# A stack of four graph layers on one core: ScalarE applies layer 2's normalisation too, and the guard of the row sums becomes the bias of their square root

## What is computed

```python
x = _layernorm(x + _L0(x, adj, nodemask, ...))   # two-layer MLP of ((1+eps) x + aggregated x)
x = _layernorm(x + _L1(x, adj, adj, ...))        # relu([x, aggregated x / deg] @ W + b)
x = _layernorm(x + _L2(x, adj, ...))             # below
x = _layernorm(x + _L3(x, adj, ...))             # MLP per edge, normalised, summed over the edges

# _layernorm:  (x - mean) / sqrt(var + eps)
# _L2:
adj_self = adj + I
rowsum = adj_self.sum(axis=2)                    # deg + 1
d = rowsum ** (-0.5);  d = where(isinf(d), 0, d)
out = (adj_self * d[:, :, None] * d[:, None, :]) @ (x @ weight) + bias
```

## Time and profile before

| | |
|---|---|
| runs shown | 545.76 us median of 3 (543.46 to 546.49) |
| the profiled execution | 544.14 us, its span 542.4 us |
| mean granted TensorE clock | 0.976 |
| busy, share of the span | PE 89%, PEld 76%, DVE 86%, ACT 66%, POOL 74% |
| instructions | PE 3299, DVE 1739, ACT 904, POOL 603 |
| first part | from the start to about 256 us |
| second part | from there to the end, a store of `out` every 8.4 us in the middle |

### The profile page before, as it was taken

One profiled execution on the slowest core, in us unless ns is written; L12 is line 12 of the kernel. 1 busy time (PEld: TensorE's weight loads), 2 busy tenths in 40 slices (PEclk: granted clock), 3 DMA queues, 4 the chain that ended last, 5 costly groups with the idle time before them and its releaser, 6 DMA issues. The chain is left out here.

```text
span 542.4 us, 13404 instructions
## 1 busy us (share of the span) xinstructions
PE 480.5 (89%) x3299; PEld 413.0 (76%) x3299; DVE 465.3 (86%) x1739; ACT 356.6 (66%) x904; POOL 401.6 (74%) x603
## 2 busy tenths in 40 slices
PE   3689998989899895975799999999999999999992
PEld 3568777778777774863689889888888888888881
DVE  5699999999999998994378998888888888888886
ACT  2256666766676673765477877776777767777773
POOL 4466666666666653644879999999999999999963
PEclk9999999999999997999699999999999999999996
DMA  5124444434333333212211222213212222122111
GB/s 187 59 70 128 127 127 128 126 126 126 126 119 118 110 121 122 75 63 90 73 49 45 89 75 57 77 55 86 76 54 77 57 83 77 53 78 60 53 40 40
DMA packets 50641, 47.49 MB, mean 88 GB/s; under 512 B 5424, under 2 KB 42288, under 8 KB 50608
## 3 DMA queue, kind: packets, MB, share of 16 engines
q1 hardware_dynamic: 50608, 47.12, 28.2%
HBM read 28.22 MB, written 18.87 MB: 87 GB/s over the span
## 5 line engine op out<-in xcount | busy, mean ns | idle before, releaser
L1353 PEld LDWEIGHTS bank<-w2c,hE 128*128 128x128 f32 x512 | 67.4, 192 | 2.0
L567 POOL TENSOR_TENSOR AD<-AD,dis 128x256 f32<-128x256 f32 x32 | 19.6, 614 | 64.6 <-DVE dis L940 64.6
L1353 PE MATMUL bank<-w2c,hE 128*128 128x128 f32 x512 | 67.4, 275 | 0.0
L1091 DVE TENSOR_REDUCE ssum<-sqE 128x4 f32<-128x512 f32 x64 | 43.5, 680 | 8.3 <-ACT sqE L786 5.0
L896 DVE TENSOR_SCALAR x<-t,mv,rstd 128x128 f32<-128x128 f32 x128 | 50.4, 434 | 0.1
L774 ACT ACTIVATE hE<-bank,const 128x512 f32<-128x512 f32 x64 | 44.1, 689 | 8.3 <-PE bank L1336 8.2
L631 POOL TENSOR_TENSOR gHu<-gH,zeros 128x256 fp32r<-128x256 f32 x64 | 45.4, 732 | 3.0 <-PE bank L1336 3.0
L572 POOL TENSOR_TENSOR bdeg<-const,sums 128x256 f32<-128x256 f32 x32 | 23.8, 744 | 31.2 <-ACT sums L693 31.2
L757 ACT ACTIVATE Qp<-bank,off 128x128 fp32r<-128x128 f32 x64 | 20.1, 364 | 40.9 <-DVE TE L1077 40.3
L676 ACT ACTIVATE std<-mv,eps_col 128x2 f32<-128x2 f32 x96 | 28.1, 293 | 28.3 <-DVE mv L886 27.0
L879 DVE BATCH_NORM_STATS2 stats<-t 128x6 f32<-128x128 f32 x192 | 45.4, 277 | 0.1
(11 more groups left out here) (168 smaller groups left out, 1659.3 us busy)
## 6 DMA issues: line engine op xcount, KB each, us to landing
hh_scratch<-hh SPq DMA_DIRECT2D x32, 256.0 KB, 2.2
gH<-hh_scratch SPq DMA_DIRECT2D x32, 256.0 KB, 2.7
IA<-adj_groups SPq DMA_DIRECT2D x32, 128.0 KB, 2.2
X<-x_groups SPq DMA_DIRECT2D x32, 128.0 KB, 2.2
AT<-adjT_groups SPq DMA_DIRECT2D x32, 128.0 KB, 2.1
res_scratch<-res SPq DMA_DIRECT2D x32, 128.0 KB, 1.7
gRES<-res_scratch SPq DMA_DIRECT2D x32, 128.0 KB, 2.0
out<-y SPq DMA_DIRECT2D x32, 128.0 KB, 2.2
```

Source lines behind the costliest of these rows:

```text
L1091: nc.vector.tensor_reduce(ssum[q][:, g * ELL:(g + 1) * ELL], sqE[g][:, :, :], AX.X, ALU.add).then_inc(b[f"ssE{g}_ready"], 1)
L1353: last = nc.tensor.matmul(ps[:, i, :], hidden[:, i * P:(i + 1) * P], w2c[:, :], start=False, stop=i == tiles - 1)
```

## The change

Layer 1 is applied on ScalarE by the same code as layer 2, from a new stage `apply(1)` at time 18.40 (5.60 in the pass, the place that `apply1` had on VectorE). VectorE gets a stage `shift_of(1)` at 18.30 (5.50) for its bias. `rs0` becomes `one`, 1 + (deg == -1), from one instruction. `rowsums` with `rsafe` goes; ScalarE takes the root of `deg` with `one` as bias, which must be a column, so it takes one instruction per graph where it took one for both. `guard_root` keeps the value where `one` is 1.

```diff
--- before.py
+++ after.py
@@ -120,14 +120,13 @@
         stats, mv = [slots(f"stats{l}_", 6) for l in range(3)], [slots(f"mv{l}_", 2) for l in range(3)]
         std = [[sb(f"std{l}_{k}", [P, GROUP]) for k in K4] for l in range(3)]
         rstd = [[sb(f"rstd{l}_{k}", [P, GROUP]) for k in K4] for l in range(3)]
-        shift = [sb(f"shift{k}", [P, GROUP]) for k in K4]
+        shift = {l: [sb(f"shift{l}_{k}", [P, GROUP]) for k in K4] for l in (1, 2)}
         maskg = [sb(f"maskg{k}", [P, GROUP]) for k in K4]
 
         sums = sb("sums", [P, SLOTS, GROUP + 1])
         deg = sums[:, :, 0:GROUP]
         rdeg = sb("rdeg", [P, SLOTS, GROUP])
-        rs0 = sb("rs0", [P, SLOTS, GROUP])
-        rsafe = sb("rsafe", [P, SLOTS, GROUP])
+        one = sb("one", [P, SLOTS, GROUP])
         rsq = sb("rsq", [P, SLOTS, GROUP])
         dis0 = sb("dis0", [P, SLOTS, GROUP])
         dis = sb("dis", [P, SLOTS, GROUP])
@@ -258,13 +257,13 @@
         x_loaded = [sem(f"x_loaded{k}") for k in K4]
         a_loaded = [sem(f"a_loaded{k}") for k in K4]
         at_loaded = [sem(f"at_loaded{k}") for k in K4]
-        names = ["a0_ready", "ai_done", "ad_ready", "sums_ready", "cnt_copied", "rs0_done", "rsafe_ready", "rsq_ready", "dis0_done", "dis_ready",
+        names = ["a0_ready", "ai_done", "ad_ready", "sums_ready", "cnt_copied", "one_ready", "rsq_ready", "dis0_done", "dis_ready",
                  "ot_ready", "unlike_done", "hT_psum", "hT_ready", "u_psum", "rT_ready", "y_psum", "mask_ready",
                  "t0_done", "stats0", "var0", "std0", "rstd0", "x1_ready",
                  "xT_psum", "xT_ready", "p_psum", "p_ready", "q_psum", "z_done",
                  "t1_done", "stats1", "var1", "std1", "rstd1", "x2_ready",
                  "gT_psum", "gT_ready", "o_psum", "xb_ready",
-                 "t2_done", "stats2", "var2", "std2", "rstd2", "shift2", "x3_ready",
+                 "t2_done", "stats2", "var2", "std2", "rstd2", "shift1", "shift2", "x3_ready",
                  "x3T_psum", "x3T_ready", "hh_psum", "hh_ready", "bdeg_done", "res_ready"]
         s = {n: sem(n) for n in names}
         stored = [sem(f"group_stored{k}") for k in K4]
@@ -684,21 +683,24 @@
 
             def root_rowsum(k, r, n):
 
-                act.wait_ge(s["rsafe_ready"], n)
-                nc.scalar.activation(rsq[:, k, :], rsafe[:, k, :], ACT.Sqrt).then_inc(s["rsq_ready"], 1)
+                act.wait_ge(s["one_ready"], n)
+                for g in range(GROUP):
+                    last = nc.scalar.activation(rsq[:, k, g:g + 1], deg[:, k, g:g + 1], ACT.Sqrt, bias=one[:, k, g:g + 1])
+                last.then_inc(s["rsq_ready"], 1)
 
             def keep_sums(k, r, n):
 
                 act.wait_ge(s["t0_done"], n)
                 nc.scalar.activation(sums[:, k, 0:GROUP], sums_ps, ACT.Copy).then_inc(s["sums_ready"], 1)
 
-            def apply2(k, r, n):
-
-                act.wait_ge(s["shift2"], n)
-                for g in range(GROUP):
-                    last = nc.scalar.activation(xn[2][k][:, g, :], t[2][k][:, g, :], ACT.Identity, bias=shift[k][:, g:g + 1],
-                                                scale=rstd[2][k][:, g:g + 1])
-                last.then_inc(s["x3_ready"], 1)
+            def apply(layer):
+                def stage(k, r, n):
+                    act.wait_ge(s[f"shift{layer}"], n)
+                    for g in range(GROUP):
+                        last = nc.scalar.activation(xn[layer][k][:, g, :], t[layer][k][:, g, :], ACT.Identity, bias=shift[layer][k][:, g:g + 1],
+                                                    scale=rstd[layer][k][:, g:g + 1])
+                    last.then_inc(s[f"x{layer + 1}_ready"], 1)
+                return stage
 
             def keep_hh(k, r, n):
                 act.wait_ge(stored[k], 32 * r + 1)
@@ -720,7 +722,7 @@
             keep_x3T = evict(x3T_ps, x3T, "x3T_psum", "x3T_ready")
             rounds(act, [(1.56, keep_hT), (2.84, relu_u), (6.46, keep_sums), (7.70, ln_std(0)), (8.24, root_rowsum),
                          (11.44, keep_xT), (13.34, keep_p), (17.42, ln_std(1)), (20.18, keep_gT), (24.88, ln_std(2)),
-                         (27.56, apply2), (29.22, keep_x3T), (31.50, keep_hh)], last=identities)
+                         (18.40, apply(1)), (27.56, apply(2)), (29.22, keep_x3T), (31.50, keep_hh)], last=identities)
 
 
             act.wait_ge(most_ready, 1)
@@ -923,12 +925,7 @@
 
                 dve.wait_ge(s["sums_ready"], n)
                 nc.vector.reciprocal(rdeg[:, k, :], deg[:, k, :])
-                nc.vector.tensor_scalar(rs0[:, k, :], deg[:, k, :], 1.0, 0.0, ALU.add, ALU.is_equal).then_inc(s["rs0_done"], 1)
-
-            def rowsums(k, r, n):
-
-                dve.wait_ge(s["rs0_done"], n)
-                nc.vector.scalar_tensor_tensor(rsafe[:, k, :], deg[:, k, :], 1.0, rs0[:, k, :], ALU.add, ALU.add).then_inc(s["rsafe_ready"], 1)
+                nc.vector.tensor_scalar(one[:, k, :], deg[:, k, :], -1.0, 1.0, ALU.is_equal, ALU.add).then_inc(s["one_ready"], 1)
 
             def inverse_root(k, r, n):
                 dve.wait_ge(s["rsq_ready"], n)
@@ -937,11 +934,11 @@
             def guard_root(k, r, n):
 
                 dve.wait_ge(s["dis0_done"], n)
-                nc.vector.scalar_tensor_tensor(dis[:, k, :], rs0[:, k, :], 0.0, dis0[:, k, :], ALU.is_equal, ALU.mult).then_inc(s["dis_ready"], 1)
+                nc.vector.scalar_tensor_tensor(dis[:, k, :], one[:, k, :], 1.0, dis0[:, k, :], ALU.is_equal, ALU.mult).then_inc(s["dis_ready"], 1)
 
             def sum1a(k, r, n):
 
-                dve.wait_ge(s["rsafe_ready"], n)
+                dve.wait_ge(s["one_ready"], n)
                 dve.wait_ge(s["q_psum"], n)
                 dve.wait_ge(s["p_ready"], n)
                 for g in range(GROUP):
@@ -964,13 +961,15 @@
                 last.then_inc(s["t2_done"], 1)
 
             stats0, var0, rstd0, apply0 = layer_norm(0)
-            stats1, var1, rstd1, apply1 = layer_norm(1)
+            stats1, var1, rstd1, _ = layer_norm(1)
             stats2, var2, rstd2, _ = layer_norm(2)
 
-            def shift2(k, r, n):
-
-                dve.wait_ge(s["rstd2"], n)
-                nc.vector.scalar_tensor_tensor(shift[k][:, :], mv[2][k][:, :, 0], -1.0, rstd[2][k][:, :], ALU.mult, ALU.mult).then_inc(s["shift2"], 1)
+            def shift_of(layer):
+                def stage(k, r, n):
+                    dve.wait_ge(s[f"rstd{layer}"], n)
+                    nc.vector.scalar_tensor_tensor(shift[layer][k][:, :], mv[layer][k][:, :, 0], -1.0, rstd[layer][k][:, :],
+                                                   ALU.mult, ALU.mult).then_inc(s[f"shift{layer}"], 1)
+                return stage
 
             def cast_counts(k, r, n):
                 if k == 0 and is_last(r):
@@ -999,10 +998,10 @@
                     nc.vector.tensor_scalar(most_i[0:1, :], most[0:1, 0:1], float(P * P), 0.0, ALU.min, ALU.max).then_inc(most_ready, 1)
 
             rounds(dve, [(0.00, mark_edges), (4.68, sum0), (6.62, stats0), (7.04, degrees), (7.20, var0),
-                         (7.36, rowsums), (8.04, rstd0), (8.30, apply0), (8.82, inverse_root), (9.28, guard_root),
+                         (8.04, rstd0), (8.30, apply0), (8.82, inverse_root), (9.28, guard_root),
                          (13.84, sum1a), (15.32, sum1b), (15.84, stats1), (16.90, var1), (18.02, rstd1),
-                         (18.40, apply1), (22.66, sum2), (23.46, stats2), (24.52, var2), (25.32, rstd2),
-                         (27.34, shift2), (28.27, cast_counts), (29.47, fullest_graph)],
+                         (18.30, shift_of(1)), (22.66, sum2), (23.46, stats2), (24.52, var2), (25.32, rstd2),
+                         (27.34, shift_of(2)), (28.27, cast_counts), (29.47, fullest_graph)],
                    last=layer3_constants, count_first=True)
```

## The result

The changed kernel takes 566.08 us (median; 564.65 to 569.12) against 545.57 for the kernel before, run beside it: a ratio of 1.040, interval 1.037 to 1.043. Its profiled execution took 564.65 us against 544.14, so 20.5 us are to be explained. The forecast was 557, with 564 as its upper end: the change is slower, as forecast, but by 9 us more.

A forecast was written before the change was run, and what follows sets the result against it. VectorE's queue was taken as the bound, 6.89 us a pass. Four passes, 4 x 7.25 + 0.8 = 29.8 against 28.0, give 27 x 0.45 = 12.2 us; with 0.5 for the drain, 544.14 becomes 556.8, forecast 557, range 546.5 to 564.

The forecast's parts named there:

- Ring A: Closed chain of waits without GpSimd, turn1 through ScalarE's apply(1) and VectorE's next pass to turn1: 7.01 us against 6.89.
- ring B: Closed chain through GpSimd, var0 over the held shift1 and apply(1) to the next var0: 7.25 us a pass; chance 0.58.
- The two roots: ScalarE's two square roots with a bias pointer, one per graph: 0.20 us each, 0.40 together.
- The turn, +0.8 a round: Where the loop turns, every fourth pass, VectorE idles before ot: 0.8 us added to four passes.
- one of the two cases: At the loop's turn, bdeg and ot come within 0.02 us: cost 0.56 if ot is first, 1.06 if bdeg is.
- Layer 2's aggregation at nothing: On TensorE, x2 is ready 2.71 us after turn1, and TensorE gets to it at 2.74 anyway: no cost.
- 20 x 0.45: Each filled pass grows by 0.45 us, from four passes with the turn taking 29.8 us against 28.0.
- 2 x 0.45 + 0.5: 0.45 us for each filled pass, plus 0.5 in the drain, where the last groups run one chain each.
- Rival 2: VectorE's shift2, one and bdeg push guard_root back: 7.40 us a pass, turn 1.06, total 564; chance 0.10.

The follow-up runs named there:

- g1: The kernel before with only the guard's lines of the diff (rs0, rsafe, one, root_rowsum, guard_root), layer 1 still applied on VectorE: 537.95 us, ratio 0.987.
- g3: The changed kernel with apply(1) behind ln_std(2) on ScalarE (18.50 for 18.40): 544.83 us, ratio 1.000.
- g5: The changed kernel with GpSimd's add_identity held until layer 1's shift of the same pass is done: 555.87 us, ratio 1.023.
- g6: The changed kernel with eight small matmuls that nobody reads on TensorE ahead of mlp0a: 561.87 us, ratio 1.031.
- g7: The changed kernel with apply(1) at 18.50, add_identity held for layer 1's shift, and one ahead of rdeg in degrees: 540.33 us, ratio 0.992.
- g8: g1 with GpSimd's add_identity waiting until layer 1 is applied on VectorE: 540.14 us, ratio 0.993.
- g10: g7 with keep_sums ahead of ln_std(2) on ScalarE (5.50 for 6.46): 550.22 us, ratio 1.011.
- g9: The changed kernel with both the held add_identity of g5 and the eight matmuls of g6: 554.7 us, ratio 1.020.

## Why the prediction was right, and where it was short

- **VectorE's queue is the bound before, partly through waits inside its instructions.** Right: `rsafe` taken away gives 6.34 us a pass, as subtracted (g1).
- **The application ahead of `ln_std(2)` closes a ring.** Right, and it is the cause: one number moves it and the time by 21 us (g3). Ring A alone was 7.01 added up and 6.97 measured (g5).
- **`shift1` waits for GpSimd; ring B, 7.25 us.** Right: 7.27. Step by step from the timeline above, `var0` to `z` 0.17, to the guard 1.63, to `AD` 2.24, its 0.72, to the application 0.06, to `std` 0.78, to `rstd` 0.32, to `var0` 1.35. The largest difference is `ot`, 0.43 for 0.40. The two roots took 0.37 (145.64 to 146.01) for the 0.40 taken. The Trainium skill ("ScalarE: Activation LUTs", section "What ACT_TABLE_LOAD costs") gave 0.38 as an estimate, and the trace agrees.
- **The turn, +0.8 a round.** Nearly: the five turns from 60 us on are 7.88 and 8.16 to 8.22, on average 0.85 over 7.27. `bdeg` was ahead of `ot`, as one of the two cases had it, but by 0.39 us, so it held `ot` for 0.07 only. What took its place was VectorE's idle time of issue, grown from 0.48 to 0.81 us, which the prediction had left as it was.
- **Layer 2's aggregation at nothing.** Right: `x` is done 2.73 us after turn1 began, and its matmul begins 2.83 after it (150.59, 150.69 against 147.86), without a wait.
- **The step that failed** is the sentence "The granted clock is 1.00, so a throttle is no part of the question". It read a state of the kernel before as a given of the changed one, and so the sum has no term for the clock. A ring that binds leaves TensorE with more idle time too, and at the turn this came to 1.31 us in one piece (TensorE was busy 2.33 of 3.2 us there before, 1.86 after). From 57.55 to 212.22 us, 20 passes of five rounds, the changed kernel took 154.7 us against 140.0. Of these 14.7, 20 x 0.45 = 9.0 were forecast. Of the missing 5.7 the four falls of the clock cost 4.2, by comparison with the same passes in g6. The rest is 0.5 for the first round's long pass, 0.4 for the 0.02 of a pass, 0.2 for the turns and 0.2 for the other passes behind them; what is left is rounding. With the filler, and so without these falls, the kernel takes 561.87 us (g6), inside the stated range.
- **The rest of the shortfall** has no such cause. The sum was 7.8 us short on the profiled execution. The five passes ahead of the 20 grew by 1.6 us for 2.3 forecast. What lies outside the 25 filled passes grew by 4.2 us (0.5, 2.2 and 1.5 above), where 2 x 0.45 + 0.5 = 1.4 had been forecast. From the last filled pass to the last group's start the clock was low for 10 us in the changed kernel and for 7 in g6, yet both took 36.8 to 36.9 us there, so the longer low stretch isn't the reason. This part stays open.

TensorE's row behind the turn of the kernel before, for the comparison above:

```profile
146.90:150.10 3.20, 2.33 (x18) 1.89 (x16) 3.20 (x18) 1.67 (x7) 1.67 (x3) 1.00 0.48 164
```

- **Rival 2** (more collisions, 564) had nearly the right time for the wrong reason: `shift2` and `one` were not held in the undisturbed passes, which took 7.27 us and not 7.40.

## What to carry to other kernels

In a pipeline of in-order queues, work moved to a less busy engine is paid at the place where it stands: look at which instruction ends up behind it there, and add up the closed chain through that instruction before counting busy time. A stall inside an instruction (0.5 us on 2 columns) is no fixed cost: when the schedule changed it came up at another instruction in g3, g7, g8 and g10, and the only part of this change that paid was the one that removed such an instruction. When a change gives TensorE idle time, ask whether the granted clock will hold: here a gap of 1.3 us at the turn, in a stretch in which TensorE was 89% busy, was followed by a fall in four rounds of five, at 0.8 to 1.2 us each.

## What the runs showed that had not been expected

- TensorE's clock fell to its lower level for 3.4 us after an idle time of 1.31 us within a stage in which it is busy nine tenths of the time, and did so in four rounds of five; eight matmuls without use per pass (0.61 us from the first one's start to the last one's end) kept it up (g6). Whether they do so in every execution isn't shown (g9). The Trainium skill ("TensorE: Matmul & The Clock Gate", section "A second HAM failure mode: psum-queue depth-cycling") tells of another kernel whose clock went back and forth because TensorE idled often and briefly between groups of matmuls. This trace agrees that idle times of 1.31 us, one a round, can be enough.
- A turn of the loop costs VectorE idle time of its own: 0.47 to 0.54 us in the kernel before, 0.64 to 0.70 in g1, and 0.81 to 0.87 in the changed kernel and every other run (0.20 to 0.53 where the loop is entered). A wait for ScalarE just before isn't the whole of it: in g1 VectorE waits for nobody, and its turns still cost more than in the kernel before. The cause stays open.
- Collisions between VectorE and GpSimd are decided by 0.03 to 0.04 us: `one` on 2 columns takes 0.15 us, or 0.60 when `bdeg` has started 0.03 us earlier (g3); of the four attempts to order them by a wait or a place, g5 and the `one` of g7 worked for the instruction meant, g8 and g10 moved the wait elsewhere.
